# Two Sign calls of ScalarE become limiting calls of GpSimd, in a convolution, attention and expert kernel

## What is computed

```python
r = r.transpose(0, 2, 1) @ ssm_out_w.T + ssm_out_b      # for four scan directions
ys = _nan_clean(r) + s                                  # nan -> 0, +-inf -> +-10000
...
m = (m0 + m1 + m2 + m3) * 0.25
out = jnp.einsum('bchw,oc->bohw', m, outproj_w) + outproj_b[None, :, None, None]
out = _nan_clean(out)
return out + x
```

## Times and profile before

| | us |
|---|---|
| median of 3 runs | 90.0 (89.72, 90.0, 90.81) |
| the profiled execution | 89.83 |
| its span in the profile | 88.1 |
| outside the span | 1.73 |
| PE busy, PEld, DVE, ACT, POOL | 80.0, 52.1, 54.9, 56.0, 23.8 |

### The profile page before, as it was taken

How to read it: one execution, slowest core, us unless ns; L and a number is a source line. 1 busy time by engine, 2 the same in 40 slices (tenths; PEclk the granted TensorE clock), 3 DMA queues, 4 the chain that set the end, 5 groups by cost and what they waited for, 6 DMA issues and landing times.

```text
span 88.1 us, 1440 instructions
## 1 busy us (share of the span) xinstructions
PE 80.0 (91%) x428; PEld 52.1 (59%) x428; DVE 54.9 (62%) x168; ACT 56.0 (64%) x119; POOL 23.8 (27%) x50
## 2 busy tenths in 40 slices
PE   4999998989999998978996899999999979999950
PEld 1589874657484444464735388767886648556620
DVE  3006786179959954757867988894253968056370
ACT  4578715899488667657999248963990928800910
POOL 5649100002532233100205000600004504718600
PEclk9999999999999999999999999999999999999999
DMA  1999700000000000000000000000056200378001
GB/s 21 203 370 425 290 2 0 0 0 0 0 11 4 0 0 0 0 0 0 0 0 7 0 0 0 0 0 1 22 188 219 65 0 7 114 196 210 19 0 60
DMA packets 2647, 5.36 MB, mean 61 GB/s; under 512 B 432, under 2 KB 1104, under 8 KB 2512
## 3 DMA queue, kind: packets, MB, share of 16 engines
q1 hardware_dynamic: 2496, 5.19, 17.8%
q10 hardware_dynamic: 144, 0.09, 0.4%
HBM read 4.98 MB, written 0.29 MB: 60 GB/s over the span
## 4 chain that ended last, share of the span: by engine, by line
PE 75%; DVE 12%; issue 8%; POOL 1%; ACT 0%; DVEq 0%; POOLq 0%
PE psM L855 12%; PE psA L704 5%; PE psA L839 5%; PE psB L839 4%; PE psA L840 4%; PE psB L840 4%; PE psB L638 4%; PE psT L650 4%; PE psT L657 3%; PE psM L755 3%; PE psA L717 2%; PE psA L728 2%; PE psB L737 2%; PE psA L730 2%; PE psA L729 2%
## 5 line engine op out<-in xcount | busy, mean ns | idle before, releaser
L536 ACT ACTIVATE hs<-psA,early 128x512 f32<-128x512 f32 x16 | 11.1, 694 | 10.9 <-PE psA L840 8.8
L855 PE MATMUL psM<-hs,w_sb 128*64 128x256 f32 x128 | 14.9, 383 | 0.0
L855 PEld LDWEIGHTS psM<-hs,w_sb 128*64 128x64 f32 x128 | 8.8, 136 | 5.8 <-issue 1.4
L536 ACT ACTIVATE hs<-psB,early 128x512 f32<-128x512 f32 x16 | 11.1, 695 | 0.0
L1267 DVE SCALAR_TENSOR_TENSOR prod<-psM,early,wbc 128x256 f32<-128x256 f32 x16 | 7.0, 475 | 6.3 <-DMA wbc<-gate_mem 3.9
L638 PE MATMUL psB<-warm 128*128 128x512 bf16 x25 | 7.9, 449 | 1.1 <-DVE warm L969 1.1
L364 POOL TENSOR_TENSOR acc<-acc,prod 128x512 f32<-128x512 f32 x5 | 6.4, 1282 | 5.2 <-DVE prod L1267 5.0
L839 PE MATMUL psA<-xh,w_hl 128*128 128x512 f32 x16 | 6.9, 430 | 0.1
L839 PE MATMUL psB<-xh,w_hl 128*128 128x512 f32 x16 | 6.3, 395 | 0.0
L840 PE MATMUL psA<-xl,w_hl 128*128 128x512 f32 x16 | 6.3, 393 | 0.0
L840 PE MATMUL psB<-xl,w_hl 128*128 128x512 f32 x16 | 6.3, 392 | 0.0
(11 more groups left out here) (210 smaller groups left out, 183.3 us busy)
## 6 DMA issues: line engine op xcount, KB each, us to landing
wbc<-gate_mem SPq DMA_DIRECT2D x16, 128.0 KB, 3.1
w_nat<-in_w_dram SPq DMA_DIRECT2D x1, 1024.0 KB, 7.7
late<-in_late_dram SPq DMA_DIRECT2D x1, 616.0 KB, 5.6
w_sb<-in_w_dram SPq DMA_DIRECT2D x1, 512.0 KB, 8.5
ssm_in<-in_ssm_dram SPq DMA_DIRECT2D x1, 320.0 KB, 4.5
x_sb<-in_x_chan_dram SPq DMA_DIRECT2D x2, 128.0 KB, 2.5
out_dram<-fin SPq DMA_DIRECT2D x2, 128.0 KB, 2.3
early<-in_early_dram ACTq DMA_DIRECT2D x1, 89.5 KB, 2.7
```

What stands on the lines that cost most here:

```text
L536: nc.scalar.activation(hs[:, n % RING, :], hidden_bank(n), ACT.Gelu, bias=cols(V_B1 + n % (E * CK))).then_inc(S["h_ok"], 1)
L855: m = nc.tensor.matmul(psM[q * C:(q + 1) * C, bank, c0:c0 + L], w2_sb[:, s % (E * CK), :], hs[:, s % RING, q * L:(q + 1) * L], start=(k == ...
```

## The change

GpSimd computes the limits in place of ScalarE: dirs_sign is now dirs limited to -1 ... 1 (max with -1, min with 1), read from dirs in SBUF, where the sign was read from PSUM; the same for o_sign. Where dirs is finite the value isn't used; where it is infinite both forms give -1 or 1, and a nan passes line 1131 as before. Two waits of TensorE on dsign_ok became waits on dirs_ok. The order of the calls on PE, DVE, ACT and POOL is another one, and keep_clock stands in other places.

```diff
             def bad_dirs(h, k):
 
                 pool.wait_ge(S["dirs_ok"], 2 * h + k + 1)
+                nc.gpsimd.tensor_scalar(dirs_sign[:, h, k, :], dirs[:, h, k, :], -1.0, 1.0, ALU.max, ALU.min)\
+                    .then_inc(S["dsign_ok"], 1)
                 nc.gpsimd.tensor_scalar(dirs_bad[:, h, k, :], dirs[:, h, k, :], 0.0, 0.0, ALU.mult, ALU.add)\
                     .then_inc(S["dbad_ok"], 1)
...
             def bad_out(h):
                 pool.wait_ge(S["o_ok"], h + 1)
+                nc.gpsimd.tensor_scalar(o_sign[:, h, :], o_sb[:, h, :], -1.0, 1.0, ALU.max, ALU.min)\
+                    .then_inc(S["osign_ok"], 1)
...
             def ssm_out(h, k):
...
-                nc.scalar.activation(dirs_sign[:, h, k, :], bank, ACT.Sign, bias=sout_b[:, 0:1],
-                                     scale=1.0 / CLAMP).then_inc(S["dsign_ok"], 1)
...
             def conv_out(h):
...
-                nc.scalar.activation(o_sign[:, h, :], psM[:, h, 0:L], ACT.Sign, bias=out_b[:, 0:1],
-                                     scale=1.0 / CLAMP).then_inc(S["osign_ok"], 1)
...
-                pe.wait_ge(S["dsign_ok"], 2 * h + t + 1)
+                pe.wait_ge(S["dirs_ok"], 2 * h + t + 1)
...
             centered(0, 0, x_sb)
+            keep_clock(1, psB[:, 0, :])
             z_weight_product()
...
             centered(1, 1, y_sb)
-            outproj_y(0)
+            keep_clock(2, psB[:, 0, :])
             variance(1, 1)
```

More of the change, by code:

```diff
@@ L367, in _ @@
             identity()
-            mask_of_heads()
-            ones_everywhere()
             zero_borders()
             borders_less_bias()
+            small_constants()
             ssm_out_weights()
+            mask_of_heads()
             wrap_columns(0)
-            share_of_rows()
+            ones_everywhere()
+            ones_beside_values()
             bad_dirs(0, 0)
             wrap_columns(1)
+            share_of_rows()
             bad_dirs(0, 1)
-            small_constants()
             bad_dirs(1, 0)
@@ L541, in gate_tanh @@
                 nc.scalar.activation(th[:, h, :, :], ld[:, h, :, :], ACT.Tanh, scale=0.5).then_inc(S["th_ok"], 1)
+            conv_diagonal(0)
+            in_bias()
             in_weights()
-            conv_diagonal(0)
             conv_diagonal(1)
-            in_bias()
             center_squares(0, 0)
@@ L552, in _ @@
             conv_diagonal(2)
-            rsqrt(0, 1, LN_EPS_CONV)
             conv_diagonal(3)
             conv_diagonal(4)
+            rsqrt(0, 1, LN_EPS_CONV)
+            ssm_weights()
             ssm_biases()
-            ssm_weights()
             center_squares(1, 0)
+            w1_high(0)
             rsqrt(1, 0, LN_EPS_CONV)
@@ L563, in _ @@
             ssm_gate(0, 1)
+            w1_high(1)
             ssm_gate(1, 0)
-            query_weights()
+            ssm_out(0, 0)
             ssm_gate(1, 1)
-            ssm_out(0, 0)
             ssm_out(0, 1)
-            w1_high(0)
             ssm_out(1, 0)
             conv_out(0)
-            w1_high(1)
-            w1_high(2)
+            query_weights()
             ssm_out(1, 1)
@@ L579, in _ @@
             squares(0, 1)
+            query_out(0)
             head_rstd(0)
-            query_out(0)
+            w1_high(2)
             center_squares(2, 1)
@@ L584, in _ @@
             nc.scalar.preload_act_table_set("gelu_and_others")
-            w1_high(3)
+            gate_high()
             squares(1, 0)
@@ L589, in _ @@
             nc.scalar.preload_act_table_set("natural_log_exp_and_others")
-            gate_high()
+            query_out(1)
             head_rstd(1)
             nc.scalar.preload_act_table_set("gelu_and_others")
-            query_out(1)
+            w1_high(3)
             token_high(0)
             hidden_gelu(0)
+            hidden_gelu(1)
             proj_gelu(1)
-            hidden_gelu(1)
             hidden_gelu(2)
@@ L831, in hidden @@
                     pe.wait_ge(S["ret_ok"], n + 1)
-                    pe.wait_ge(S["dsign_ok"], 2 * n + 2)
+                    pe.wait_ge(S["dirs_ok"], 2 * n + 2)
                 pe.wait_ge(S["xl_ok"], h + 1)
@@ L874, in _ @@
             in_product(0)
+            ssm_bias_products()
+            variance(0, 1)
             in_product(1)
-            variance(0, 1)
-            ssm_bias_products()
             convolution(0, 0, 3)
@@ L891, in _ @@
             raster(0, 0)
-            query_transpose()
             raster(0, 1)
@@ L896, in _ @@
             raster(1, 1)
+            query_transpose()
+            outproj_y(0)
             outproj(0, 0)
@@ L899, in _ @@
             column(1)
+            keep_clock(2, psB[:, 0, :])
+            centered(2, 0, x1)
             outproj_y(1)
-            centered(2, 0, x1)
-            keep_clock(2, psB[:, 0, :])
             variance(2, 0)
             outproj(1, 0)
+            keep_clock(2, psB[:, 0, :])
             outproj(1, 1)
@@ L918, in _ @@
             query_product(1)
-            keep_clock(3, psB[:, 0, :])
+            keep_clock(2, psB[:, 0, :])
             t2_to_tokens(0)
-            keep_clock(7, psB[:, 0, :])
+            keep_clock(8, psB[:, 0, :])
             head_products(1)
@@ L1310, in _ @@
             conv_sum(1)
+            ln_weights()
+            normalise(1, 0, norm_c)
             weight_sums()
-            normalise(1, 0, norm_c)
             normalise(1, 1, norm_c)
+            w1_low(0)
             gated_u(0, 0)
+            gated_u(0, 1)
             kv_weights()
-            gated_u(0, 1)
             kv_bias_parts()
@@ L1336, in _ @@
             with_query_input(0)
-            w1_low(0)
             square_sums(1, 0)
+            gate_low()
+            tokens_after_attention(0)
             square_sums(1, 1)
-            tokens_after_attention(0)
             stats(0)
@@ L1346, in _ @@
             token_low(0)
-            gate_low()
             with_query_input(1)
@@ L1367, in _ @@
             gated_pair(3)
+            first_pair_sum()
             gated_pair(4)
-            first_pair_sum()
             gated_pair(5)
```

6 lines of the change are left out of this document (2 added, 4 removed).

## The result

The changed kernel takes 95.93 us (median of 4 runs, 95.47 to 96.32) against 90.35 for the kernel before (4 runs). The ratio is 1.062, with an interval of 1.056 to 1.067: 5.6 us slower, where 91.1 was forecast and 92.2 was the end of the range. The profiled execution took 95.47, its span 93.8 (before 89.83 and 88.1), so its own difference is 5.6 too.

What follows compares the result with a forecast made beforehand. The prediction took TensorE, three quarters of the chain, as the bound. Its terms, 0.22 + 0.43 + 0 + 0 + 0.35 + 0.1 = 1.1 us, on a median of 90.0 gave 91.1, range 89.8 to 92.2.

Steps and rivals of the forecast that it cites:

- What the limit costs in its place: GpSimd's limit at each scan output, taken as 0.62 us; with holds, 0.55 more per output that TensorE waits for.
- The holds: GpSimd and two-tile VectorE calls keep each other out until the first ends; cleaning takes 0.55 more instead of 0.19.
- Step 1: One filling matmul ahead of z_weight_product, where TensorE never waits, paid in full: +0.22.
- Steps 2 and 3: outproj_y(0) and query_transpose moved on TensorE, +0.43; outproj of half 0, +0.2 to -0.18, taken as 0.
- Step 2: query_transpose leaves the rasters, -0.11, and stands with outproj_y(0) behind the last raster, +0.54: together +0.43.
- the slow rival: Holds add up at half 0's outputs: late gated_u, (0, 1)'s limit starting behind 25.9, +2.1, 92.1 us; chance 0.16.
- Step 4: column(1) to centered(2, 0): filling matmuls replace outproj_y(1), and the 0.65 covers x1's lateness: 0.
- Steps 5 and 6: Last two products of outproj of half 1, +0.35; query_out(1) ahead of head_rstd(1), about +0.1.
- step 7: Extra filling matmuls between the halves of outproj and later lie in waits; without those waits each costs 0.21.
- That line 1235 would be held again: Ahead of the second gate, its 1.08 should recur; otherwise 0.9 comes back, 89.7 us; with fewer holds, chance 0.18.
- ScalarE as the bound: Fast rival: 3.1 us leave ScalarE; if all were on the path, the time would be 87.5 us; chance 0.04.

Runs made afterwards that it cites:

- The first experiment: The kernel after, in its own order, with GpSimd's two limiting calls written as times 0, plus 0; 92.21 us against 90.64, ratio 1.021.

## Why the prediction was wrong

**The step that failed** is "What the limit costs in its place". It took 0.62 "since form, type and size are those of that row", and put the upper end at the two-input sum, 1.27. The row was of the same instruction but of other operations, and for one-input calls of GpSimd the operations decide: 1.91 to 2.23 us in the kernel after, 1.93 alone. The wrong term is therefore 1.3 us or more at each wide call. At the last output, dirs to clean took 2.15 before and was forecast at 2.70; it is 3.95. At output (0, 1) the limit starts at 26.20 and is held a little itself, and column(1) comes 3.4 us late where 0.65 was forecast. The first experiment, which gives the call the forecast length, takes 3.7 us away: of the 3.5 between the two profiled spans 1.5 lie ahead of column(1), 1.3 between it and keys_values, 0.3 from there to hidden(0) and 0.4 behind. This one term is most of the gap between 91.1 and 95.9. The prediction said that nothing showed max and min on GpSimd, and that another length of theirs would prove it wrong. Yet it never carried its own upper end into the range: 0.65 more at each of the two waits would have made 92.4, already beyond 92.2, and the measured length is beyond that end too. An unknown operation needed an end at several times 0.62.

**The page that spoke against the change** was set aside too easily. The Trainium skill, "GPSIMD Engine Reference", section "Engine selection", wants elementwise max on VectorE, and its factor of two is for calls with two inputs; with that factor the prediction worked out 92.6. The row of 0.62 was no evidence against it, being of other operations. The measured ratio of the two engines for this limit, which has one input, is 1.93 to 0.42, or 4.6. The page's "1-input is roughly line-rate" can fit the 0.62 and 0.61 of three pairs of operations and the copy here, and not the 1.49 to 1.94 of all the others.

**The holds were right** for a call of 0.62. Line 1134 was forecast at "reported at 1.1" beside the product, and takes 1.02; it takes 0.70 without it. Forecast was that it ends 0.6 behind the product's end: 37.94 against 37.40. The general form, that whichever comes first keeps the other out until it ends, was read from three short meetings, and one of them (ln_kbv) is of a call that reads one tile, not two. Beside a limit of 2.09 it fails: line 1107 ran there at its full speed.

**Step 1** (+0.22) is right: the convolution starts 0.46 later in the profiled execution, of which 0.22 is the filling matmul. The remaining 0.2 is the scatter of the start, described below. **Steps 2 and 3** were wrong in kind and in size. Step 2 priced outproj_y(0) and the transpose at 0.54 of TensorE's time; putting them back gave nothing that can be seen, since TensorE waited for output (0, 1) in their place. The real cost was for the most part the one that the slow rival named: gated_u of half 1 late, then the cleaning of (0, 0), then a limit for (0, 1) that starts after 25.9 (26.24 in the first experiment, where TensorE also waits 0.42 for gated_u(1, 0) itself). Its reason for the late gated_u is wrong, though: kv_bias_parts stands wholly ahead of it in both kernels, and in the run that brought it forward again as well. What that run put back are kv_weights, w1_low(0) and w1_high(1). The first experiment has column(1) at 29.71; it began its convolution 0.53 later than the kernel before, so 1.3 of its 1.8 us are this stretch's, three times the 0.43 of steps 2 and 3. **Step 4** was right for calls of 0.62: from column(1) to centered(2, 0) the first experiment took 3.24 for 3.27; with the slow limit it is 3.70, since x1 of half 0 comes late. **Steps 5 and 6** came out right in size: from column(1) to keys_values the first experiment took 6.97 for 6.65, +0.32 for a forecast of 0.35; from keys_values to hidden(0) 16.38 for 16.32, +0.06 for 0.1. What query_out does in it was not tried by itself, and neither was step 7.

**The rivals.** The slow one had most of the mechanism for what the first experiment leaves, a late gated_u and the delay that runs on from it, but it too was priced with 0.62 (92.1). That line 1235 would be held again was right: 1.08 in both (line 1238 after). ScalarE as the bound is refuted: it lost 2.6 us and nothing came of them, nor in the two runs that gave the limit to VectorE.

**A cost that stood nowhere** is the clock. It took nothing from the kernel after (mean 0.999), but in the old order the same substitution lost up to 3.3 us more, by one wait of TensorE that was 1 us longer. The last 0.4 us of the 5.6 lie behind hidden(0): the gates' rows arrived for prod at 83.67, 5.67 later than before, and TensorE waited 0.36 for it. The two DMA round trips in front of it began 5.31 later; why they took longer is open.

## What to carry to other kernels

Price a GpSimd call by a row with the same operations; the same instruction, type and size is not enough. Ask of every moved call who runs beside it: line 1131 took 1.0 to 1.1 us for 0.7 when it began just behind the start of GpSimd's product (0.6 to 0.8), and a copy of 30 columns on GpSimd that began beside line 1131 took 0.54 for 0.21. And where a wait of TensorE grows by 1 us, look at the clock behind it too.

## What the hardware showed that I had not expected

- One-input calls of GpSimd on 128x512 f32: 0.62 us for times and plus, plus and times, times twice; 0.61 for a copy; 1.93 to 1.94 for six other pairs; 1.49 to 1.50 for max, min, times, plus and greater or equal alone. A multiplication with an addition behind it is thus 2.4 times as fast as the multiplication alone. At 256 columns max and min take 1.07.
- Beside a limit of 2.09 us a two-tile VectorE instruction that began 1.27 us after it took 0.27, as with GpSimd idle (0.28), where one that began 0.35 after it took 1.02 for 0.74.
- TensorE's granted clock went to 0.50 behind a wait of 3.1 us in the profiled execution of one program, and stayed at 1.00 behind one of 2.1 us in another.
- Kernels with the same code up to there begin the convolution at anything from 8.07 to 9.20 us in their one profiled execution. Half of it is one group: the first products behind the opening filling matmuls take between 0.55 and 1.06 us (first the run with the limit on VectorE, then that with the move of ln_weights alone):

```profile
4.50 0.55 PE psT L646 x2
```

```profile
4.50 1.06 PE psT L650 x2
```

The convolution starts correspondingly later, 8.07 in the one and 9.06 in the other. Whoever compares profiles of single executions should take such a start off first.
